# A graph network on one core: one-hot rows of the histogram stage laid out tile by tile, and half of one of them built on ScalarE

## The chip, the cores and the metric

The kernel runs on one core of a Trainium2 chip. The metric is device time in microseconds for one execution. The kernel before was timed three times: median 5992.08 us, 5985.56 to 5997.7 us. TensorE multiplies, VectorE and ScalarE work elementwise, GpSimd here mostly issues indirect DMAs, and a sync engine issues plain DMAs. Each engine runs its own instruction stream, and the streams meet at semaphores.

## The reference

Four graph layers run in sequence over the same graph: 6250 nodes with 128 features, and 106250 edges sorted by destination. A layer normalization and a relu stand ahead of each layer. What matters here is only how the graph is used. Layer 0, cut to its sum:

```
h = x @ w_in + b_in
Wij = (ssp(f_ij @ w_f1 + b_f1) @ w_f2 + b_f2) * rcut_ij[:, None]
x_ij = h[idx_j] * Wij
agg = segment_sum(x_ij, idx_i)
```

Layer 1 (a graph convolution) needs the sum of the edge weights at each destination node:

```
deg = segment_sum(ew, dst)
dinv = where(deg > 0, rsqrt(deg), 0.0)
norm = dinv[src] * ew * dinv[dst]
```

To sum by source, the kernel sorts the edges by source on the chip. For that it first counts how many edges each source node has.

## The kernel before

A node number is split into a block (number divided by 128, 49 blocks) and a lane (the remainder, 0 to 127). The edges lie in 832 tiles of 128, one edge per partition. Eight tiles are a group (`G = 8`), so there are 104 groups.

The stages follow one another, each with semaphores of its own, and a barrier of all engines stands between two of them. The first is `setup` (L125). The second is `histograms` (L201), which the change touches; after it come `rows_of_ends`, layer norm statistics, node tables, and the edge stage of layer 0, `filter_edges` (L621).

The histogram stage makes two results from one loop over the 104 groups, written as 52 turns of two halves `h`:

- The counts by source. For each tile there is a one-hot matrix of the source's block, `oh_hi` (128 edges by 49), and one of its lane, `oh_lo` (128 edges by 128). Their product over the edges, added up over all 832 tiles in the PSUM tile `p_count`, holds the count of edges of every source node. Before, `oh_lo` is the stationary operand and `oh_hi` the moving one, so `p_count` is lane by block (128x49). After the loop it is copied out and transposed to block by lane.
- The weight sums by destination. `d_lo` is the one-hot of the destination's lane. For each tile it is multiplied by six columns `w3` (the edge weight for the tile's first block or the next, each split in three bf16 parts). ScalarE copies the result of a group, 48 columns, from `p_deg` into `parts` (`keep`, L395).

VectorE makes all three one-hots of a group (L270, L272, L274): it compares a table of lane numbers with the node numbers. `oh_lo` and `d_lo` are stored lane-major, `[P, 2, P, G]`: the eight tiles of a group lie side by side for each lane. The table for that, `lanes16`, holds each lane number eight times (L177), and one tile's one-hot is read by TensorE at a stride of eight elements. `oh_hi` is stored tile-major.

Order and waits: VectorE may start group g once the weight sums of group g - 2 have left TensorE (`free`). TensorE waits for `oh_lo` (`src_hot`), multiplies eight tiles of counts (L347), waits for `d_lo` (`dst_hot`) and for ScalarE's copy of group g - 2 (`deg_kept`), and multiplies eight tiles of sums (L352). ScalarE waits for these and copies.

After the loop VectorE takes the counts (L277, L279), scans them (L280), and reduces `parts` (L287). The sync engine loads all weights during the loop (L386). GpSimd has nothing to do in this stage.

In `filter_edges` the same one-hots of the source are made again, tile-major, by `source_hots` (L832):

```
nc.vector.tensor_tensor(out=oh_lo[:, h], in0=K.lane16[:].unsqueeze(1).broadcast_to([P, G, P]),
                        in1=K.src_lo16[:, cols].unsqueeze(2).broadcast_to([P, G, P]), op=ALU.is_equal).then_inc(hot_ready, 1)
```

ScalarE's rows that the prediction uses are these forms: L510 is a Relu with bias and scale both read per partition; L782 and L784 are an Abs and a Relu of a PSUM tile with such a bias; L788 is an Ln of an SBUF tile with such a bias; L803 is a scaled copy from PSUM with such a scale.

Of the kernel before, what the change touches and what calls it, by code (L numbers as in the profile page):

```python
# [23 lines left out]
BF16 = mybir.dt.bfloat16  # L24
# [7 lines left out]
P = 128  # L32
# [6 lines left out]
G = 8  # L39
# [85 lines left out]
def setup(nc, A, K, s):  # L125

    loaded, made, tidy, blank, lanes = s.sem("loaded"), s.sem("made"), s.sem("tidy"), s.sem("blank"), s.sem("lanes")
    with nc.Block() as block:
# [29 lines left out]
        def _(dve):  # L158
# [18 lines left out]
            nc.vector.tensor_copy(K.lanes16[:], K.lane[:].unsqueeze(2).broadcast_to([P, P, G]))  # L177
# [5 lines left out]
            nc.vector.tensor_copy(K.dst_lo16[:], K.low_i[:])  # L183
            nc.vector.tensor_copy(K.dst_blk[0:1, :], K.key_i[0:1, :])
# [16 lines left out]
def histograms(nc, K, Dr, A, s):  # L201
# [4 lines left out]
    oh_lo = s.sb("oh_lo", [P, 2, P, G], BF16)  # L206
    d_lo = s.sb("d_lo", [P, 2, P, G], BF16)
    by_lane = s.sb("by_lane", [P, NB])
# [18 lines left out]
    src_hot, dst_hot, free, lane_counts, counts_turned = s.sem("src_hot"), s.sem("dst_hot"), s.sem("free"), s.sem("lane_counts"), s.sem("counts_turned")  # L227
# [15 lines left out]
    with nc.Block() as block:  # L243
        @block.vector
        def _(dve):
# [20 lines left out]
            with nc.vector.Fori(0, NG // 2) as i:  # L266
                for h in range(2):
                    cols = bass.ds(i * 2 * G + h * G, G)
                    dve.wait_ge(free, i * 2 + h + 1)
                    nc.vector.tensor_tensor(out=oh_hi[:, h], in0=K.lane16[:, 0:NB].unsqueeze(1).broadcast_to([P, G, NB]),  # L270
                                            in1=K.src_hi16[:, cols].unsqueeze(2).broadcast_to([P, G, NB]), op=ALU.is_equal)
                    nc.vector.tensor_tensor(out=oh_lo[:, h], in0=K.lanes16[:],  # L272
                                            in1=K.src_lo16[:, cols].unsqueeze(1).broadcast_to([P, P, G]), op=ALU.is_equal).then_inc(src_hot, 1)
                    nc.vector.tensor_tensor(out=d_lo[:, h], in0=K.lanes16[:],  # L274
                                            in1=K.dst_lo16[:, cols].unsqueeze(1).broadcast_to([P, P, G]), op=ALU.is_equal).then_inc(dst_hot, 1)
            dve.wait_ge(summed, 1)
            nc.vector.tensor_copy(by_lane[:], p_count[:, 0:NB]).then_inc(lane_counts, 1)  # L277
            dve.wait_ge(counts_turned, 1)
            step(dve, nc.vector.tensor_copy(count[:], p_count[0:NB, P:2 * P]), 1)  # L279
# [50 lines left out]
        def _(pe):  # L330
            pe.sem_inc(free, 2)
            pe.wait_ge(zeroed, 1)
            nc.tensor.matmul(p_count[:, 0:NB], zero[:], zero[:, 0:NB], start=True, stop=False, skip_group_check=True)
# [57 lines left out]
        def _(act):  # L391
# [2178 lines left out]
```

## Time and profile before

| | |
|---|---|
| median of three runs | 5992.08 us |
| the profiled execution, its own time | 5992.08 us |
| its span, first to last instruction | 5990.8 us |
| histogram loop in the trace | 32 to 211 us |
| VectorE busy in 32 to 210.7 us | 177.16 of 178.7 us |
| TensorE busy there | 163.49 us |
| ScalarE busy there | 20.55 us |

The profiled execution took 1.3 us more than its span. Busy time is time in which an instruction was under way on the engine; on VectorE and ScalarE consecutive instructions overlap by a little, so a sum of durations is more than the time that passes, and the distance between two starts is the better measure of what an instruction costs in a row of others. `hist_`, `c_`, `e_` and `k_` ahead of a tile's name say in which stage's memory it lies.

### The profile page before, as it was taken

What the parts mean: (1) busy time and instruction counts of PE and PEld (TensorE: products, weight loads), DVE (VectorE), ACT (ScalarE), POOL (GpSimd) and SP (SyncE); (2) the same over time, 40 slices, a digit from 0 to 9 for tenths busy, and PEclk for the clock granted to TensorE, in tenths of its full rate; (3) what the DMA queues carried; (4) which work ended last, traced back from release to release, by engine and by line L of the source; (5) the groups of instructions that cost most, each with busy time, mean ns of one, the idle gap of its engine ahead of it and who ended that gap; (6) DMA issues with size and microseconds to landing.
All of it is one profiled execution on the core that took longest, in us unless ns stands there. A gap on an engine that the chain in (4) does not pass through costs nothing. (4 is left out here: it accounts for less than half of the span.)

```text
span 5990.8 us, 102085 instructions
## 1 busy us (share of the span) xinstructions
PE 3458.2 (58%) x21282; PEld 2671.2 (45%) x21283; DVE 3512.1 (59%) x8519; ACT 1720.2 (29%) x3922; POOL 3789.8 (63%) x3879
## 2 busy tenths in 40 slices
PE   7768888888797333333354444444146645556556
PEld 7646666666575333333342222222136534344434
DVE  9858888888697433333355555555554454444444
ACT  0235555555344000000022333333157621111112
POOL 0077777777572677777707777777235437777774
PEclk9779999999897555555575555555579978766787
DMA  3099999999462121122228999999657622222221
GB/s 93 17 256 274 276 281 283 279 286 281 124 156 69 54 53 52 53 53 52 53 71 282 290 291 291 291 291 291 127 162 202 177 63 57 58 58 58 58 58 53
DMA packets 937028, 939.38 MB, mean 157 GB/s; under 512 B 330232, under 2 KB 777930, under 8 KB 936842
## 3 DMA queue, kind: packets, MB, share of 16 engines
q1 hardware_dynamic: 770906, 549.05, 34.0%
q0 software_dynamic: 137776, 369.86, 19.3%
q10 hardware_dynamic: 28288, 19.84, 1.1%
q8 instruction: 20, 0.33, 0.0%
q14 instruction: 38, 0.31, 0.0%
HBM read 686.22 MB, written 252.06 MB: 157 GB/s over the span
## 5 line engine op out<-in xcount | busy, mean ns | idle before, releaser
L1583 POOL DMA_INDIRECT edges_kv<-kv,edges_idx x880 | 836.5, 951 | 408.3 <-issue 267.8
L951 POOL DMA_INDIRECT by_src<-edges_rows,edges_pos x832 | 899.2, 1081 | 268.0 <-issue 257.2
L2213 POOL DMA_INDIRECT sum_rows<-table,sum_idx x832 | 806.2, 969 | 348.6 <-issue 253.2
L1310 POOL DMA_INDIRECT sum_rows<-table,sum_idx x832 | 788.1, 947 | 367.7 <-issue 251.4
L1387 PE MATMUL sum_p_sum<-sum_hot,sum_rows 128*128 128x128 f32 x1664 | 388.4, 427 | 662.4 <-DMA sum_rows<-table,sum_idx 662.4
L1387 PEld LDWEIGHTS sum_p_sum<-sum_hot,sum_rows 128*128 128x128 f32 x1664 | 360.4, 329 | 690.6 <-issue 690.6
L2311 PE MATMUL sum_p_sum<-sum_hot,sum_msg 128*128 128x128 f32 x1664 | 370.4, 414 | 466.7 <-DVE a_acc L2272 460.5
L1682 DVE TENSOR_TENSOR edges_kv<-edges_kv,edges_p_e 128x512 f32<-128x512 f32 x440 | 282.7, 684 | 530.4 <-DMA edges_kv<-kv,edges_idx 514.5
L2311 PEld LDWEIGHTS sum_p_sum<-sum_hot,sum_msg 128*128 128x128 f32 x1664 | 344.4, 315 | 552.9 <-issue 552.9
L1366 DVE TENSOR_TENSOR a_acc<-a_acc,sum_p_sum 128x128 f32 x832 | 234.3, 282 | 547.6 <-PE sum_p_sum L1387 546.4
L723 PE MATMUL edges_p_attr<-k_wekv,edges_attr 128*128 128x256 f32 x1664 | 467.0, 429 | 118.4 <-ACT edges_rows L798 114.6
L1713 PE MATMUL edges_p_q<-q_q,edges_src_hotT 128*128 x2640 | 373.0, 286 | 109.7 <-issue 86.7
L2257 DVE TENSOR_TENSOR sum_msg<-sum_p_msg,sum_rows 128x512 f32<-128x512 f32 x208 | 133.9, 685 | 493.5 <-DMA sum_rows<-table,sum_idx 493.5
L723 PEld LDWEIGHTS edges_p_attr<-k_wekv,edges_attr 128*128 128x128 f32 x1664 | 335.7, 212 | 174.6 <-ACT edges_rows L798 125.4
L1896 POOL TENSOR_TENSOR sum_wv<-sum_vv,sum_wv 128x1024 f32<-128x1024 f32 x110 | 212.5, 1932 | 313.6 <-ACT sum_wv L1911 312.1
L1623 ACT COPY edges_p_e<-edges_ekv 128x512 f32<-128x512 f32 x440 | 258.8, 589 | 463.6 <-DVE edges_kv L1682 446.6
L798 ACT COPY edges_rows<-edges_p_attr 128x512 f32<-128x512 f32 x416 | 223.4, 585 | 538.5 <-DMA by_src<-edges_rows,edges_pos 508.0
L1713 PEld LDWEIGHTS edges_p_q<-q_q,edges_src_hotT 128*128 128x128 bf16 x2640 | 274.8, 104 | 231.0 <-issue 172.9
L1349 DVE TENSOR_SCALAR sum_hot<-k_lane,k_dst_f,k_ew 128x128 f32<-128x128 f32 x832 | 304.2, 367 | 88.8 <-issue 88.3
L1723 PE MATMUL edges_p_l<-k_ident,edges_score 128*64 128x128 f32 x110 | 43.2, 392 | 498.7 <-DVE edges_score L1690 498.7
L1325 ACT COPY sum_idx<-k_src_i 128x8 int32 (+1 forms) x104 | 20.2, 197 | 989.9 <-DMA sum_rows<-table,sum_idx 984.0
L2272 DVE TENSOR_TENSOR a_acc<-a_acc,sum_p_sum 128x128 f32 x832 | 239.2, 288 | 99.6 <-DVE a_acc L2272 6.3
(381 smaller groups left out, 7781.6 us busy)
## 6 DMA issues: line engine op xcount, KB each, us to landing
edges_ekv<-by_src SPq DMA_DIRECT2D x110, 1024.0 KB
v<-edges_kv SPq DMA_DIRECT2D x110, 512.0 KB, 4.1
sum_vv<-v SPq DMA_DIRECT2D x110, 512.0 KB, 4.0
edges_attr<-in_attr128T SPq DMA_DIRECT2D x104, 512.0 KB
edges_near<-h_in SPq DMA_DIRECT2D x832, 48.0 KB
sum_rows<-by_src SPq DMA_DIRECT2D x110, 264.0 KB, 3.0
edges_src_b<-rel SPq DMA_DIRECT2D x110, 256.0 KB
edges_dst_b<-dst SPq DMA_DIRECT2D x104, 256.0 KB
```

The lines of the kernel that those rows point to most:

```text
L723: mm = nc.tensor.matmul(p_attr[:, c % 2, j, :], attr[:, q, (2 * c + j) * P:(2 * c + j + 1) * P], K.wekv[:], start=True, stop=True)
L951: nc.gpsimd.indirect_dma_start(Dr.by_src0, bass.IndirectOffsetOnAxis(pos[:, q, j:j + 1], 0), rows[:, q % 2, j, :], None).then_inc(scattere ...
L1310: nc.gpsimd.indirect_dma_start(rows[:, q, j, :], None, Dr.table, bass.IndirectOffsetOnAxis(idx[:, q, j:j + 1], 0)).then_inc(fetched[q], 16)
L1349: ins = nc.vector.tensor_scalar(hot[:, h, j, :], K.lane[:, 0:P], to, weight, ALU.is_equal, ALU.mult)
L1387: mm = nc.tensor.matmul(p_sum[:, c, j % 4, :], rows[:, q, j, :], hot[:, h, j, :], start=True, stop=True)
L1583: nc.gpsimd.indirect_dma_start(kv[:, q, j, :], None, Dr.kv, bass.IndirectOffsetOnAxis(idx[:, q, j:j + 1], 0)).then_inc(fetched[q], 16)
L1623: nc.scalar.copy(p_e[:, c % 2], ekv[:, q, 2 * c:2 * c + 2, :]).then_inc(e_ready, 1)
L1682: nc.vector.tensor_tensor(out=both, in0=both, in1=p_e[:, c % 2], op=ALU.add).then_inc(kv_ready, 1)
L1713: mm = nc.tensor.matmul(p_q[:, h, c, j % C, :], shot[:, h, j * P:(j + 1) * P], K.q[:, bass.ds(blk[j], 1), k, :].rearrange("p a d -> p (a d)"),
L2213: nc.gpsimd.indirect_dma_start(rows[:, q, j, :], None, Dr.table, bass.IndirectOffsetOnAxis(idx[:, q, j:j + 1], 0)).then_inc(fetched[q], 16)
L2272: nc.vector.tensor_tensor(out=place, in0=place, in1=p_sum[h][:, j // 4, j % 4, :], op=ALU.add).then_inc(added, 1)
L2311: mm = nc.tensor.matmul(p_sum[h][:, c, j % 4, :], msg[:, h, j, :], hot[:, h, j, :], start=True, stop=True)
```

## The change

The one-hots `oh_lo` and `d_lo` become tile-major, `[P, 2, G, P]`, so that a tile's one-hot is contiguous. The lane table that they are compared with is the plain 128-element one, repeated over the tiles, and the node numbers are repeated along the last dimension. `lanes16` and its making go.

In the count product the operands change places: `oh_hi` (49 columns) is stationary and `oh_lo` (128 columns) moves, so `p_count` is block by lane as it is needed, and the copy and the transpose behind the loop go.

VectorE makes `d_lo` for the first four tiles of a group only. For the other four ScalarE computes max(0, 1 - |lane - destination lane|), which is 1 where they are equal and 0 elsewhere: four Abs with the negated destination lane as bias into `far`, a wait for them, and one Relu of 512 columns (`near`). The negated lanes, `minus_lo`, are made once in the set-up. TensorE waits for both makers (`near_ready` is new). ScalarE makes its part of group g + 1 ahead of its copy for group g.

```diff
-            nc.vector.tensor_copy(K.lanes16[:], K.lane[:].unsqueeze(2).broadcast_to([P, P, G]))
...
             nc.vector.tensor_copy(K.dst_hi[:], K.key_i[:])
             nc.vector.tensor_copy(K.dst_lo16[:], K.low_i[:])
+            nc.vector.tensor_scalar(K.minus_lo[:], K.low_i[:], -1.0, None, ALU.mult)
             nc.vector.tensor_copy(K.dst_blk[0:1, :], K.key_i[0:1, :])
...
-    oh_lo = s.sb("oh_lo", [P, 2, P, G], BF16)
-    d_lo = s.sb("d_lo", [P, 2, P, G], BF16)
-    by_lane = s.sb("by_lane", [P, NB])
+    oh_lo = s.sb("oh_lo", [P, 2, G, P], BF16)
+    d_lo = s.sb("d_lo", [P, 2, G, P], BF16)
+    far = s.sb("far", [P, 2, G // 2, P])
...
                     cols = bass.ds(i * 2 * G + h * G, G)
+                    half = bass.ds(i * 2 * G + h * G, G // 2)
                     dve.wait_ge(free, i * 2 + h + 1)
                     nc.vector.tensor_tensor(out=oh_hi[:, h], in0=K.lane16[:, 0:NB].unsqueeze(1).broadcast_to([P, G, NB]),
                                             in1=K.src_hi16[:, cols].unsqueeze(2).broadcast_to([P, G, NB]), op=ALU.is_equal)
-                    nc.vector.tensor_tensor(out=oh_lo[:, h], in0=K.lanes16[:],
-                                            in1=K.src_lo16[:, cols].unsqueeze(1).broadcast_to([P, P, G]), op=ALU.is_equal).then_inc(src_hot, 1)
-                    nc.vector.tensor_tensor(out=d_lo[:, h], in0=K.lanes16[:],
-                                            in1=K.dst_lo16[:, cols].unsqueeze(1).broadcast_to([P, P, G]), op=ALU.is_equal).then_inc(dst_hot, 1)
+                    nc.vector.tensor_tensor(out=oh_lo[:, h], in0=K.lane16[:].unsqueeze(1).broadcast_to([P, G, P]),
+                                            in1=K.src_lo16[:, cols].unsqueeze(2).broadcast_to([P, G, P]), op=ALU.is_equal).then_inc(src_hot, 1)
+                    nc.vector.tensor_tensor(out=d_lo[:, h, 0:G // 2], in0=K.lane16[:].unsqueeze(1).broadcast_to([P, G // 2, P]),
+                                            in1=K.dst_lo16[:, half].unsqueeze(2).broadcast_to([P, G // 2, P]), op=ALU.is_equal).then_inc(dst_hot, 1)
             dve.wait_ge(summed, 1)
-            nc.vector.tensor_copy(by_lane[:], p_count[:, 0:NB]).then_inc(lane_counts, 1)
-            dve.wait_ge(counts_turned, 1)
-            step(dve, nc.vector.tensor_copy(count[:], p_count[0:NB, P:2 * P]), 1)
+            step(dve, nc.vector.tensor_copy(count[:], p_count[0:NB, 0:P]), 1)
...
-                        nc.tensor.matmul(p_count[:, 0:NB], oh_lo[:, h, :, j], oh_hi[:, h, j, :], start=False, stop=False, skip_group_check=True)
+                        nc.tensor.matmul(p_count[0:NB, 0:P], oh_hi[:, h, j, :], oh_lo[:, h, j, :], start=False, stop=False, skip_group_check=True)
                     pe.wait_ge(dst_hot, i * 2 + h + 1)
+                    pe.wait_ge(near_ready, i * 2 + h + 1)
                     pe.wait_ge(deg_kept, i * 2 + h + 1)
                     pe.sem_inc(tick, 1)
                     for j in range(G):
-                        mm = nc.tensor.matmul(p_deg[:, h, j * 6:(j + 1) * 6], d_lo[:, h, :, j],
+                        mm = nc.tensor.matmul(p_deg[:, h, j * 6:(j + 1) * 6], d_lo[:, h, j, :],
                                               w3[:, bass.ds(i * 2 * G + h * G + j, 1), :, :].rearrange("p a r m -> p (a r m)"), start=True, stop=True)
                     mm.then_inc(free, 1)
             pe.wait_ge(free, NG + 2)
             pe.sem_inc(summed, 1)
-            pe.wait_ge(lane_counts, 1)
-            nc.tensor.transpose(p_count[0:NB, P:2 * P], by_lane[:], K.ident[:]).then_inc(counts_turned, 1)
...
+            def near(g, h):
+
+                act.wait_ge(free, g + 1)
+                for j in range(G // 2):
+                    ins = nc.scalar.activation(far[:, h, j, :], K.lane[:], ACT.Abs, bias=K.minus_lo[:, bass.ds(g * G + G // 2 + j, 1)])
+                ins.then_inc(far_ready, 1)
+                act.wait_ge(far_ready, g + 1)
+                nc.scalar.activation(d_lo[:, h, G // 2:G, :], far[:, h], ACT.Relu, bias=K.ones[:, 0:1], scale=-1.0).then_inc(near_ready, 1)
+
             def keep(g, h):
...
-            with nc.scalar.Fori(0, NG // 2) as i:
+            near(0, 0)
+            with nc.scalar.Fori(0, NG // 2 - 1) as i:
                 for h in range(2):
+                    near(i * 2 + h + 1, 1 - h)
                     keep(i * 2 + h, h)
+            near(NG - 1, 1)
+            for h in range(2):
+                keep(NG - 2 + h, h)
```

VectorE's stream in one half of a turn of the histogram loop, with the shape that is written (`e_lane` is `lane16`, `c_lanes` is `lanes16`), before:

```order
L270 ISA
L270 TENSOR_TENSOR hist_oh_hi<-e_lane,e_src_hi 128x392
L272 REGISTER_ALU
L272 TENSOR_TENSOR hist_oh_lo<-c_lanes,e_src_lo 128x1024
L274 REGISTER_ALU
L274 TENSOR_TENSOR hist_d_lo<-c_lanes,c_dst_lo 128x1024
```

The same place now:

```order
L271 ISA
L271 TENSOR_TENSOR hist_oh_hi<-e_lane,e_src_hi 128x392
L273 REGISTER_ALU
L273 TENSOR_TENSOR hist_oh_lo<-e_lane,e_src_lo 128x1024
L275 REGISTER_ALU
L275 TENSOR_TENSOR hist_d_lo<-e_lane,c_dst_lo 128x512
```

There are still three compares per group; the second reads the other lane table, the third too and is half as long.

ScalarE's stream from its table load to the end of the first half of a loop turn, before:

```order
L393 ACT_TABLE_LOAD
L400 UNCONDITIONAL_BRANCH
L400 ISA
L398 ISA [waits hist_free]
L398 COPY hist_parts<-hist_p_deg 128x48
```

The first half of a loop turn now:

```order
L397 ISA [waits hist_free]
L397 ACTIVATE hist_far<-k_lane,c_minus_lo 128x128
L397 ISA
L397 ACTIVATE hist_far<-k_lane,c_minus_lo 128x128
L397 ISA
L397 ACTIVATE hist_far<-k_lane,c_minus_lo 128x128
L397 ISA
L397 ACTIVATE hist_far<-k_lane,c_minus_lo 128x128
L400 ACTIVATE hist_d_lo<-hist_far,k_ones 128x512 [waits hist_far]
L404 REGISTER_ALU
L405 ISA [waits hist_free]
L405 COPY hist_parts<-hist_p_deg 128x48
```

Five activations of the next group now stand ahead of each copy, and no table load stands among them.

## Rows read from the trace of the kernel before

**Rows 1.** The page: span; busy us (share) xinstructions of each engine.
```profile
span 5990.8 us, 102085 instructions
...
PE 3458.2 (58%) x21282; PEld 2671.2 (45%) x21283; DVE 3512.1 (59%) x8519; ACT 1720.2 (29%) x3922; POOL 3789.8 (63%) x3879
```

**Rows 2.** Busy time by stretch: start:end us, length, each engine, TensorE clock, DMA share, GB/s.
```profile
32.00:210.70 178.70, 163.49 (x1664) 157.80 (x1664) 177.16 (x313) 20.55 (x103) 0.00 (x0) 1.00 0.15 39
210.70:233.00 22.30, 10.80 (x51) 8.13 (x51) 15.09 (x32) 2.59 (x5) 0.00 (x0) 0.83 0.00 1
233.00:300.00 67.00, 41.90 (x178) 36.68 (x178) 53.24 (x176) 20.77 (x57) 0.00 (x0) 0.50 0.15 40
900.00:1530.00 630.00, 533.73 (x4180) 394.47 (x4178) 524.30 (x1673) 345.31 (x906) 486.49 (x453) 0.95 0.93 274
3139.00:4249.00 1110.00, 485.99 (x2964) 319.42 (x2964) 583.86 (x866) 326.87 (x760) 836.49 (x880) 0.50 0.92 285
```

**Rows 3.** The histogram loop's groups, 32 to 211 us; columns as the page's part 5.
```profile
L352 PE MATMUL hist_p_deg<-hist_w,hist_d_lo 128*128 x832 | 110.8, 220 | 0.1
...
L347 PE MATMUL hist_p_count<-hist_oh_hi,hist_oh_lo 128*128 128x49 bf16 x832 | 72.2, 241 | 25.4 <-issue 13.8 <-DVE hist_oh_lo L272 11.7
L272 DVE TENSOR_TENSOR hist_oh_lo<-c_lanes,e_src_lo 128x1024 bf16<-128x1024 bf16 x104 | 71.1, 684 | 0.0
L274 DVE TENSOR_TENSOR hist_d_lo<-c_lanes,c_dst_lo 128x1024 bf16<-128x1024 bf16 x104 | 71.1, 684 | 0.0
...
L270 DVE TENSOR_TENSOR hist_oh_hi<-e_lane,e_src_hi 128x392 bf16<-128x392 bf16 x104 | 58.6, 563 | 0.0
L398 ACT COPY hist_parts<-hist_p_deg 128x48 f32 x104 | 20.7, 200 | 174.2 <-PE hist_p_deg L352 174.2
```

**Rows 4.** Timeline of the loop, 207 to 212 us: start us, us, engine, line, what.
```profile
207.36 0.20 ACT L398 COPY hist_parts<-hist_p_deg 128x48 f32 x1 [1.47 <-PE hist_p_deg L352]
207.40 0.56 DVE L270 TENSOR_TENSOR hist_oh_hi<-e_lane,e_src_hi 128x392 bf16<-128x392 bf16 x1
...
207.49 0.69 PE L347 MATMUL hist_p_count<-hist_oh_hi,hist_oh_lo 128*128 128x49 bf16 x8 [0.27 <-issue]
207.88 0.68 DVE L272 TENSOR_TENSOR hist_oh_lo<-c_lanes,e_src_lo 128x1024 bf16<-128x1024 bf16 x1
...
208.01 0.96 PE L352 MATMUL hist_p_deg<-hist_w,hist_d_lo 128*128 x8
208.48 0.68 DVE L274 TENSOR_TENSOR hist_d_lo<-c_lanes,c_dst_lo 128x1024 bf16<-128x1024 bf16 x1
...
209.10 0.20 ACT L398 COPY hist_parts<-hist_p_deg 128x48 f32 x1 [1.54 <-PE hist_p_deg L352]
...
209.46 1.17 PE L352 MATMUL hist_p_deg<-hist_w,hist_d_lo 128*128 x8
210.76 0.21 DVE L277 COPY hist_by_lane<-hist_p_count 128x49 f32<-128x49 f32 x1 [1.60 <-PEq L356]
210.78 0.20 ACT L398 COPY hist_parts<-hist_p_deg 128x48 f32 x1 [1.48 <-PE hist_p_deg L352]
...
211.51 0.28 DVE L279 COPY hist_count<-hist_p_count 49x128 f32<-49x128 f32 x1 [0.54 <-PE hist_p_count L358]
```

**Rows 5.** Waits of ScalarE and of the DMA-issuing queue, start to 234 us.
```profile
ACT hist_parts L398 <- PE hist_p_deg L352: 172.7, 103, 19.4
...
SPq L243 <- PEq L243: 160.2, 1, 160.2
```

**Rows 6.** One line each, L272 and L837: durations ns min/median/max, first and last start.
```profile
L272 DVE TENSOR_TENSOR hist_oh_lo<-c_lanes,e_src_lo x104: 680/684/687, 32.5 to 207.9; 128x1024 bf16<-128x1024 bf16 x104
...
L837 DVE TENSOR_TENSOR edges_src_lo_hot<-e_lane,e_src_lo x104: 1209/1218/1222, 307.9 to 1503.6; 128x1024 bf16<-128x1024 bf16 x104
```

**Rows 7.** Timeline of VectorE in the edge loop, around 1503 us.
```profile
1503.09 0.56 DVE L835 TENSOR_TENSOR edges_src_hi_hot<-e_lane,e_src_hi 128x392 bf16<-128x392 bf16 x1
1503.57 1.22 DVE L837 TENSOR_TENSOR edges_src_lo_hot<-e_lane,e_src_lo 128x1024 bf16<-128x1024 bf16 x1
1504.70 0.48 DVE L844 TENSOR_SCALAR edges_dst_hotT<-edges_dst_b,k_node_col 128x1024 bf16<-128x1024 bf16 x1
```

**Rows 8.** ScalarE's groups over the whole span, shapes apart.
```profile
L1623 ACT COPY edges_p_e<-edges_ekv 128x512 f32<-128x512 f32 x440 | 258.8, 589 | 463.6 <-DVE edges_kv L1682 446.6 <-DMA edges_src_b<-rel 11.0 <-ACT edges_logit L1616 4.3
...
L1923 ACT COPY sum_p_sum<-sum_none 128x408 f32<-128x408 f32 x222 | 111.4, 502 | 85.5 <-DVE den_sums L1970 74.0 <-DVE sum_none L1952 7.9
...
L788 ACT ACTIVATE edges_ln<-edges_mag,k_ones 128x512 f32<-128x512 f32 x104 | 75.1, 722 | 3.4
...
L510 ACT ACTIVATE nodes_h<-k_x,k_shift,k_rstd 128x128 f32<-128x128 f32 x98 | 38.8, 481 | 6.3 <-PE nodes_p_t L551 4.1 <-PEq L487 2.2
```

**Rows 9.** Timelines of ScalarE: 257 us, and 423 to 428 us.
```profile
257.40 4.72 ACT L510 ACTIVATE nodes_h<-k_x,k_shift,k_rstd 128x128 f32<-128x128 f32 x12 [1.10 <-PEq L487]
...
423.67 1.77 ACT L803 ACTIVATE edges_w_cut<-edges_p_w,k_ew 128x64 f32<-128x64 f32 x8
425.25 0.76 ACT L782 ACTIVATE edges_mag<-edges_p_z,k_b_f 128x512 f32<-128x512 f32 x1
425.82 0.77 ACT L784 ACTIVATE edges_relu<-edges_p_z,k_b_f 128x512 f32<-128x512 f32 x1
426.39 0.71 ACT L786 ACTIVATE edges_mag<-edges_mag 128x512 f32<-128x512 f32 x1
427.14 0.72 ACT L788 ACTIVATE edges_ln<-edges_mag,k_ones 128x512 f32<-128x512 f32 x1
427.77 1.05 ACT L798 COPY edges_rows<-edges_p_attr 128x512 f32<-128x512 f32 x2
```

**Rows 10.** Timeline of TensorE at 3302 us, clock 0.50: 128-column moving rows.
```profile
3302.71 3.49 PE L1713 MATMUL edges_p_q<-q_q,edges_src_hotT 128*128 x24 [1.05 <-issue]
```

**Rows 11.** Timeline of VectorE in the set-up, 11 to 14 us.
```profile
11.10 0.68 DVE L177 CAST c_lanes<-k_lane 128x1024 bf16<-128x1024 f32 x1
11.70 0.58 DVE L179 TENSOR_SCALAR c_key_i<-k_dst_i 128x832 int32<-128x832 int32 x1
...
13.33 0.59 DVE L183 CAST c_dst_lo<-c_low_i 128x832 bf16<-128x832 int32 x1
13.83 0.57 DVE L184 COPY k_dst_blk<-c_key_i 1x832 int32<-1x832 int32 x1
```

More of the change, by code:

```diff
@@ L226, in histograms @@
     p_count, p_small, p_deg = s.ps("p_count", [P, 512]), s.ps("p_small", [P, 512]), s.ps("p_deg", [P, 2, 512])
-    src_hot, dst_hot, free, lane_counts, counts_turned = s.sem("src_hot"), s.sem("dst_hot"), s.sem("free"), s.sem("lane_counts"), s.sem("counts_turned")
+    src_hot, dst_hot, far_ready, near_ready, free = s.sem("src_hot"), s.sem("dst_hot"), s.sem("far"), s.sem("near"), s.sem("free")
     deg_kept, split, tick = s.sem("deg_kept"), s.sem("split"), s.sem("tick")
@@ L332, in _ @@
             pe.wait_ge(zeroed, 1)
-            nc.tensor.matmul(p_count[:, 0:NB], zero[:], zero[:, 0:NB], start=True, stop=False, skip_group_check=True)
+            nc.tensor.matmul(p_count[0:NB, 0:P], zero[:, 0:NB], zero[:], start=True, stop=False, skip_group_check=True)
             pe.wait_ge(blk_row, 1)
@@ L2476, in build @@
                 K.key_i, K.low_i = c.sb("key_i", [P, T], I32), c.sb("low_i", [P, T], I32)
-                K.dst_hi, K.dst_lo16 = c.sb("dst_hi", [P, T]), c.sb("dst_lo16", [P, T], BF16)
-                K.lanes16 = c.sb("lanes16", [P, P, G], BF16)
+                K.dst_hi, K.minus_lo, K.dst_lo16 = c.sb("dst_hi", [P, T]), c.sb("minus_lo", [P, T]), c.sb("dst_lo16", [P, T], BF16)
                 with Space(nc, "setup") as s:
```

## The prediction

> **What bounds the kernel now.** I read the page first: 5990.8 us of span, with no engine over 63% busy [rows 1]. That average covers stages with different limits, and the change touches one only, so the second view is the table of busy time by stretch. In the histogram loop, 32 to 210.7 us, VectorE is busy 177.16 of 178.70 us, TensorE 163.49, ScalarE 20.55 and GpSimd not at all [rows 2]. VectorE has no gap there, so it is the bound, with TensorE not far behind.
>
> The third view is the groups of the loop. VectorE has three compares per group, 104 of each, of 563, 684 and 684 ns, each with 0.0 us of idle time ahead of it [rows 3]. Their sum, 1.93 us, is more than what passes, because instructions in a row overlap. The timeline shows what each costs from start to start: 207.40 to 207.88 is 0.48 us for `oh_hi`, then 0.60 us to 208.48 for `oh_lo` [rows 4]. `d_lo` takes the same 684 ns, so about 0.61. That is 1.69 us. Over the loop, the first `oh_lo` starts at 32.5 and the last at 207.9 [rows 6], so 175.4 us over 103 groups is 1.703 us per group. I use 1.703: the three compares and about 0.01 us of loop turn.
>
> ScalarE waits for TensorE's sums 172.7 of these 179 us [rows 5]; it has much time to give. The sync engine's loads are not late: its queue then waits 160.2 us at the stage's barrier for others [rows 5]. Stages are parted by barriers, so whatever this loop loses or wins goes into the total one to one, unless a later stage changes its own pace.
>
> **The compares in the new layout.** This is the term that decides. VectorE's `oh_hi` isn't changed: 0.48 us. The new `oh_lo` doesn't stand in this loop's trace, but it stands in the edge loop's: L837 has the same operands, the same tile-major output, and the node number repeated along the last dimension. It takes 1218 ns (1209 to 1222, 104 times), against 684 ns (680 to 687) for the lane-major form of the same 1024 elements [rows 6]. From its start to the next instruction is 1503.57 to 1504.70, 1.13 us, against 0.60 [rows 7, 4]. Could L837 be slow because of what runs beside it, such as GpSimd's indirect DMAs? Its neighbour L835 has the form of `oh_hi` and takes 0.56 us there and 0.56 us here, where GpSimd is idle [rows 7, 4, 2]; and L837's spread of 13 ns over a long stage with all kinds of neighbours shows no such share. So the layout costs +0.53 us per group.
>
> The new `d_lo` on VectorE has the same form with 512 elements. The line through 560 ns at 392 and 1218 ns at 1024 elements [rows 7, 6] has 1.04 ns per element; 512 elements come to 0.685 us, less the 0.08 us by which L835's duration is more than its distance of 0.48: 0.60 us. Its ends: half of 1.13 is 0.57 (no fixed part), and 0.48 x 512 / 392 is 0.63 (nothing but a fixed rate). I take 0.60, the line between two rows of its own form. So halving `d_lo` wins nothing: half the elements at about twice the price each.
>
> Together: 0.48 + 1.13 + 0.60 + 0.01 = 2.22 us per group, against 1.703. From unrounded numbers I take 2.22; ends 2.19 and 2.25. Times 104 groups: +53.8 us, ends +50.6 and +56.9.
>
> **ScalarE's new part.** Per group four Abs of 128 columns with one per-partition bias, a wait for them, a Relu of 512 columns, and the old copy. The nearest row for a 512-column activation from SBUF with one such operand is L788, 722 ns; copies of 512 and 408 columns take 589 and 502 ns, 0.837 ns per column [rows 8]. An Abs of 128 columns is then 722 - 384 x 0.837 = 401 ns. Two activations from SBUF in a row overlap by 0.096 us: 12 of L510 take 4.72 us, so (4.72 - 0.48) / 11 = 0.385 apart, at 481 ns each [rows 9, 8]. So an Abs every 0.305 us: 3 x 0.305 + 0.401 = 1.32. The wait for its own result costs 0.04 (426.39 + 0.71 = 427.10, next start 427.14), the Relu 0.63 until the next start (427.14 to 427.77) [rows 9], and the copy 0.200 - 0.096 = 0.10 [rows 3]. Sum: 2.09 us per group. That is under VectorE's 2.22, so it is hidden, but by 0.13 us only.
>
> Its ends. Below: eight of L803, 64 columns, take 1.77 us, 0.204 apart, and 64 more columns make 0.257; with the 0.57 us between L782 and L784 for the Relu [rows 9] it is 0.77 + 0.40 + 0.04 + 0.57 + 0.10 = 1.89. Above: L510 itself, the only 128-column activation from SBUF, at 0.385 and 0.481, though it reads two per-partition operands, and no overlap elsewhere: 1.16 + 0.48 + 0.04 + 0.72 + 0.20 = 2.60. I take 2.09, whose terms have the right number of operands. The register step ahead of each Abs costs nothing extra: L803 has one too, at 0.204 us.
>
> Here the Trainium skill bears on the choice. L510 shows 481 ns and L788 722 ns [rows 8]. "ScalarE: Activation LUTs", in its section on what ACT_TABLE_LOAD costs, says that an activation with one per-partition pointer takes about 280 ns + 0.833 ns per column, that each further pointer adds about 93 ns, and that those in a row overlap by about 93 ns. By that, as an estimate, L510 is 480 and L788 706, so the trace agrees within 16 ns; an Abs is 387, one every 294, and the group 3 x 0.294 + 0.387 + 0.04 + 0.61 + 0.10 = 2.02. Neither it nor my rows make ScalarE the bound; only L510's spacing, taken over with its second operand, would.
>
> Does ScalarE's turn fit in time? Its part for group g + 2 may start when the sums of group g are done and copied, about 1.2 us after VectorE's `d_lo` of g (208.48 + 0.68 = 209.16, sums end at 210.63 [rows 4]; with the count product in front, up to 1.5). It is done 2.0 us later, at +3.5 at most, and TensorE needs it when VectorE's `d_lo` of g + 2 is ready, at +4.4. So TensorE's new wait is nearly always met. What queues behind it, the sums, `free` and so VectorE's group g + 3, has 0.9 us of room.
>
> **TensorE.** Before: 0.69 us for eight count products, 0.96 to 1.17 for eight sums [rows 4]. Now the count product moves 128 columns, not 49, over 49 columns of weights. The nearest row of 128 moving bf16 columns is L1713, at clock 0.50 (1.2 GHz): 24 in 3.49 us, (3.49 - 0.29) / 23 = 0.139 us each [rows 10, 2]. Eight: 1.11 us at most; at the clock of 1.00 (2.4 GHz) that the loop has [rows 2] nearer the 0.69 of now. The sums read contiguous weights and get no slower: at most 1.17. Together 1.65 to 2.28; I take 1.8, hidden under 2.22. Relief for TensorE wins nothing, as it isn't the bound.
>
> **Small terms.** Behind the loop the copy and the transpose go: `count` is taken at the time of `by_lane`, so 211.51 - 210.76 = -0.75 us, all on the path [rows 4]. In the set-up the lane table goes (11.10 to 11.70, -0.60) and `minus_lo` comes, 832 elements as L183 (13.33 to 13.83, +0.50) [rows 11]: -0.10.
>
> **Sum.** +53.8 - 0.75 - 0.10 = +53.0 us on the profiled execution's 5992.08 us, which is also the median of the runs: 6045 us, +0.9%.
>
> **Rivals.**
> 1. *ScalarE becomes the bound.* For: its sum lies only 0.13 us under VectorE's, and it has semaphore and register steps in the chain. Against: it needs the second operand's price, or 0.04 us per instruction more than I count. With L510's spacing alone: 1.16 + 0.40 + 0.04 + 0.63 + 0.10 = 2.33 us, times 104 against 1.703 is +65.2, so 6056. At its upper end of 2.60, +93.3, so 6084. TensorE's upper end of 2.28 would lead to 6051 in the same way.
> 2. *Not slower: the new layout keeps the old rate.* Place: the compare of 1024 elements. If it took 0.60 us here and its half about 0.35, VectorE would need 1.44 us, and the loop's pace would pass to ScalarE and TensorE. It would end level with before where these reach 1.70: TensorE can (1.65); ScalarE only if an Abs comes every 0.204 us as L803 does, 0.61 + 0.34 + 0.04 + 0.57 + 0.10 = 1.66. Then 5991. Against: L837's 1209 to 1222 ns, 104 times, and ScalarE's lower end of 1.89, with which this still costs +19 and ends at 6011.
> 3. *A later stage gives it back or adds to it.* TensorE does less in this loop, and its clock afterwards could be another. Against: the clock falls to 0.50 behind the loop now, in 233 to 300 us, and is 0.95 in the long edge loop [rows 2]; there is nothing left to gain there. A few us either way.
>
> **How the numbers follow.** Forecast 0.74; rival 1, 0.20; rival 2, 0.03; rival 3 with more than 40 us, 0.03, half of it to either side. The forecast's own range is +50 to +57 from the loop, with 6 us for the spread of runs: 6037 to 6054. The range given, 6036 to 6068, takes in most of rival 1 and leaves out its upper end. A measurement of this kernel can tell about 0.2% (12 us) from no change. Faster 0.015, same 0.03, slower 0.955.
>
> **What would show it.** In the new trace: `oh_lo` at 1.21 to 1.22 us and the half `d_lo` at 0.67 to 0.70; VectorE still without gaps, about 2.22 us per group; durations on ScalarE that add up to about 2.5 us per group (overlaps counted twice), waiting a little for TensorE's sums each time; the loop from 32 to about 264 us; `near_ready` hardly waited for. If VectorE waits for `free` in each group and ScalarE has no wait, rival 1 is right. If `oh_lo` takes 0.69, the main term is wrong.

## The result, and the profile after

The changed kernel takes 6040.28 us (median of 6 runs, 6035.44 to 6043.26) against 5991.54 us before (6 runs, 5984.08 to 5997.7). The ratio is 1.008 with a 95% interval of 1.0068 to 1.0091: slower by 49 us, 41 to 55. The forecast was 6045 us, or +53.

The profiled execution took 6046.61 us, +54.5 to the one before. Its page, span and busy time by engine [rows 1]:

```profile
span 6045.4 us, 103159 instructions
...
PE 3497.4 (58%) x21281; PEld 2674.7 (44%) x21282; DVE 3568.2 (59%) x8518; ACT 1911.0 (32%) x4442; POOL 3799.9 (63%) x3879
```

By stretch, as in [rows 2]: the loop, the two stretches behind it, and the long edge loop, 55 us later than before:

```profile
32.00:264.00 232.00, 203.42 (x1664) 158.49 (x1664) 230.71 (x313) 209.88 (x613) 0.00 (x0) 1.00 0.12 31
264.00:287.00 23.00, 13.55 (x52) 11.04 (x51) 13.15 (x25) 2.59 (x5) 0.00 (x0) 1.00 0.00 1
287.00:354.00 67.00, 41.89 (x178) 36.67 (x178) 53.34 (x180) 20.76 (x57) 0.00 (x0) 0.60 0.14 37
955.00:1585.00 630.00, 544.20 (x4143) 401.83 (x4139) 522.23 (x1662) 340.89 (x893) 486.62 (x449) 0.93 0.93 272
```

Two things are to be seen. VectorE is busy 230.71 of 232 us in a loop that was 178.7 us long, and ScalarE went from 20.55 to 209.88 us. Little moved elsewhere: TensorE's clock is still 1.00 in the loop, and 0.93 in the long edge loop, where it was 0.95. Behind the loop it stays up for longer, 1.00 and then 0.60 where 0.83 and 0.50 were granted before [rows 2], but no time came of it (see below).

The loop's groups [rows 3], from 15 to 290 us, columns as in the page's part 5:

```profile
L397 ACT ACTIVATE hist_far<-k_lane,c_minus_lo 128x128 f32<-128x128 f32 x416 | 132.8, 391 | 12.8 <-issue 12.8
L273 DVE TENSOR_TENSOR hist_oh_lo<-e_lane,e_src_lo 128x1024 bf16<-128x1024 bf16 x104 | 127.1, 1222 | 0.0
L346 PE MATMUL hist_p_count<-hist_oh_lo,hist_oh_hi 128*49 128x128 bf16 x832 | 109.0, 311 | 38.7 <-DVE hist_oh_lo L273 38.7
...
L400 ACT ACTIVATE hist_d_lo<-hist_far,k_ones 128x512 bf16<-128x512 f32 x104 | 75.1, 722 | 3.4
L275 DVE TENSOR_TENSOR hist_d_lo<-e_lane,c_dst_lo 128x512 bf16<-128x512 bf16 x104 | 71.6, 689 | 0.0
```

`oh_lo` went from 684 to 1222 ns, and half a `d_lo` costs 689 ns where the whole cost 684. VectorE has still 0.0 us of idle time ahead of each compare. A stretch of the loop [rows 4], start and duration in us:

```profile
121.37 1.22 DVE L273 TENSOR_TENSOR hist_oh_lo<-e_lane,e_src_lo 128x1024 bf16<-128x1024 bf16 x1
...
121.91 0.72 ACT L400 ACTIVATE hist_d_lo<-hist_far,k_ones 128x512 bf16<-128x512 f32 x1
122.50 0.69 DVE L275 TENSOR_TENSOR hist_d_lo<-e_lane,c_dst_lo 128x512 bf16<-128x512 bf16 x1
122.55 0.20 ACT L405 COPY hist_parts<-hist_p_deg 128x48 f32 x1
...
122.73 1.05 PE L346 MATMUL hist_p_count<-hist_oh_lo,hist_oh_hi 128*49 128x128 bf16 x8 [0.30 <-DVE hist_oh_lo L273]
123.01 1.28 ACT L397 ACTIVATE hist_far<-k_lane,c_minus_lo 128x128 f32<-128x128 f32 x4 [0.26 <-issue]
123.11 0.56 DVE L271 TENSOR_TENSOR hist_oh_hi<-e_lane,e_src_hi 128x392 bf16<-128x392 bf16 x1
123.58 1.22 DVE L273 TENSOR_TENSOR hist_oh_lo<-e_lane,e_src_lo 128x1024 bf16<-128x1024 bf16 x1
...
123.71 0.95 PE L352 MATMUL hist_p_deg<-hist_w,hist_d_lo 128*128 x8
```

VectorE's starts are 1.13 us (`oh_lo` to `d_lo`), 0.61 (`d_lo` to `oh_hi`) and 0.47 apart: 2.21 us per group. All 104 `oh_lo`, with durations in ns (min/median/max) and the first and last start [rows 6]:

```profile
L273 DVE TENSOR_TENSOR hist_oh_lo<-e_lane,e_src_lo x104: 1218/1222/1224, 32.8 to 260.9; 128x1024 bf16<-128x1024 bf16 x104
```

So (260.9 - 32.8) / 103 = 2.215 us per group, against 1.703. Behind the loop [rows 4]:

```profile
264.31 0.28 DVE L278 COPY hist_count<-hist_p_count 49x128 f32<-49x128 f32 x1 [1.60 <-PEq L356]
...
265.51 5.34 DVE L286 TENSOR_REDUCE hist_by_tile<-hist_parts 128x1664 f32<-128x4992 f32 x1
```

The same reduction in the kernel before:

```profile
212.71 5.33 DVE L287 TENSOR_REDUCE hist_by_tile<-hist_parts 128x1664 f32<-128x4992 f32 x1
```

It starts at 265.51 us against 212.71: +52.8 us up to there. From its start to the end of the span it is 5779.9 us against 5778.1: the later stages add no more than 1.8 us.

The waits from 40 to 250 us, with the total, the number and the longest:

```profile
PE hist_p_count L346 <- DVE hist_oh_lo L273: 24.5, 95, 0.3
...
ACT hist_far L397 <- issue: 12.0, 47, 0.3
```

TensorE waits for `oh_lo` in every group. ScalarE has no wait for TensorE in the list, only 0.26 us of "issue" (waiting for nothing that the profile shows) in every second group. `near_ready` holds nobody: the Relu of the group whose sums start at 121.42 us had ended at 120.61.

### The profile page after: what moved, and what is told of

Read it like the earlier page. It is cut to its first block and busy times, and to the rows that moved or that the text cites. A ratio compares the mean times of both kernels' runs of the same rounds, so it can differ in the third digit from the quotient of the medians.

```text
span 6045.4 us, 103159 instructions
## 1 busy us (share of the span) xinstructions
PE 3497.4 (58%) x21281; PEld 2674.7 (44%) x21282; DVE 3568.2 (59%) x8518; ACT 1911.0 (32%) x4442; POOL 3799.9 (63%) x3879
## 5 line engine op out<-in xcount | busy, mean ns | idle before, releaser
L1378 DVE TENSOR_TENSOR a_acc<-a_acc,sum_p_sum 128x128 f32 x832 | 235.6, 283 | 549.3 <-PE sum_p_sum L1399 548.2
L2013 PE MATMUL sum_p_sum<-sum_wv,sum_hot 128*128 128x136 f32 x1760 | 235.8, 288 | 107.5 <-ACT sum_p_sum L1935 59.0
```

The costliest lines, as they stand in the source:

```text
L2013: mm = nc.tensor.matmul(p_sum[:, h, c, bass.ds(slot[j], 1), :].rearrange("p a f -> p (a f)"), hot[:, h, j, :], wv[:, q, j, :], start=False ...
```

## Experiments

For each, the pace of the loop is worked out as above: the first and the last start of `oh_lo`, over 103 groups. The table has it beside the times, all medians in us.

| run | us per group | time before the same runs | time | ratio, 95% |
|---|---|---|---|---|
| before | 1.703 | | 5991.54 | |
| changed | 2.215 | 5991.54 | 6040.28 | 1.0080 (1.0068 to 1.0091) |
| layout only | 2.748 | 5994.40 | 6101.36 | 1.0180 (1.0164 to 1.0195) |
| half only | 3.593 | 5994.40 | 6184.94 | 1.0320 (1.0304 to 1.0336) |
| five on ScalarE | 2.396 | 5994.40 | 6067.70 | 1.0127 (1.0111 to 1.0142) |
| two on ScalarE, lane-major | 2.099 | 5994.40 | 6028.94 | 1.0060 (1.0046 to 1.0073) |
| swap only | 2.503 | 5980.69 | 6066.26 | 1.0143 (1.0126 to 1.0160) |
| pairs in the changed kernel | 2.004 | 5993.11 | 6026.30 | 1.0053 (1.0037 to 1.0068) |
| pairs, old operands, two on ScalarE | 1.674 | 5993.11 | 5984.06 | 0.9986 (0.9977 to 0.9995) |
| pairs for `oh_hi` only | 1.606 | 5993.11 | 5983.92 | 0.9987 (0.9978 to 0.9996) |

The kernel before was timed again with each series of runs, and the series ran on different chips, so times are compared within a row only. The pace before comes from one trace. The pace accounts for the time to within 6.3 us: for "layout only" (2.748 - 1.703) x 103 = 107.6 us, measured 107.0; for "swap only" 82.4, measured 85.6; for "pairs in the changed kernel" 31.0, measured 33.2; for "five on ScalarE" 71.4, measured 73.3; for "pairs for `oh_hi` only" -10.0, measured -9.2. It is 4 to 6 us off for the changed kernel (52.7, measured 48.7), "half only" (194.7, measured 190.5), "two on ScalarE, lane-major" (40.8, measured 34.5) and "pairs, old operands" (-3.0, measured -9.1). What differs there behind the loop was not looked for.

**Layout only.**

```diff
-  d_lo[:, h, 0:G // 2] compared on VectorE; d_lo[:, h, G // 2:G] made by near()
+  d_lo[:, h] compared on VectorE, tile-major, 1024 elements
-                    pe.wait_ge(near_ready, i * 2 + h + 1)
```

> The changed kernel with ScalarE's part taken out: VectorE makes all eight tiles of d_lo in the tile-major layout, TensorE waits for it alone, ScalarE only copies. Theory (VectorE sets the pace, and the layout doubles the price of a compare): 0.48 + 1.13 + 1.13 + 0.01 = 2.75 us per group against 1.703, so +109 us less 0.75 behind the loop: 6100 us, 60 us over the changed kernel. Rival (the layout is not what costs, ScalarE's part set the changed kernel's pace): the loop gets no slower than the changed kernel's 2.21 us per group, or falls back to about 1.7: 5990 to 6040 us.

VectorE's timeline:

```profile
120.54 1.22 DVE L273 TENSOR_TENSOR hist_oh_lo<-e_lane,e_src_lo 128x1024 bf16<-128x1024 bf16 x1
121.67 1.22 DVE L275 TENSOR_TENSOR hist_d_lo<-e_lane,c_dst_lo 128x1024 bf16<-128x1024 bf16 x1
122.81 0.56 DVE L271 TENSOR_TENSOR hist_oh_hi<-e_lane,e_src_hi 128x392 bf16<-128x392 bf16 x1
```

Both compares take 1.13 us from start to start, and 2.748 us per group and +107 us were measured where 2.75 and 6100 were expected. The layout is the cost, and moving half of `d_lo` away bought back (2.748 - 2.215) x 103 = 55 us of it. This run keeps the exchanged operands of the count product too, but VectorE has no wait in it, so they have no part in its pace. Nor does ScalarE's work slow VectorE much: the median `oh_lo` takes 1215 ns here and 1222 ns beside it.

**Half only.**

```diff
+  d_lo[:, h, :, 0:G - S] compared on VectorE, lane-major, S = 4
+  nc.scalar.activation(d_lo[:, h, :, G - S:G].rearrange("p l j -> p j l"), far[:, h], ACT.Relu, ...)
+                    pe.wait_ge(near_ready, i * 2 + h + 1)
```

> The kernel before with ScalarE's part alone: lane-major layout and its tables stay, VectorE compares the first four tiles of d_lo (512 elements), ScalarE makes the other four as in the changed kernel but writes them at a stride of eight elements. VectorE then needs about 0.48 + 0.61 + 0.35 = 1.44 us per group and ScalarE sets the pace, so this measures ScalarE's own pace. Theory (ScalarE has slack in the changed kernel, 2.02 to 2.09 us per group): +33 to +40 us, 6025 to 6032 us. Rival (the changed kernel's ScalarE has no slack, its idle 0.26 us at every second group is the loop's turn and not a wait): 2.21 us per group, +52 us, 6044 us, the same as the changed kernel. If half a d_lo on ScalarE were free: 5991 or less.

Neither theory held. ScalarE's timeline:

```profile
119.79 0.53 ACT L413 COPY hist_parts<-hist_p_deg 128x48 f32 x1
120.00 1.30 ACT L405 ACTIVATE hist_far<-k_lane,c_minus_lo 128x128 f32<-128x128 f32 x4
121.33 2.60 ACT L408 ACTIVATE hist_d_lo<-hist_far,k_ones 128x512 bf16<-128x512 f32 x1
123.44 0.53 ACT L413 COPY hist_parts<-hist_p_deg 128x48 f32 x1
```

ScalarE does set the pace, but at 3.59 us: the Relu takes 2.60 us where the changed kernel's takes 0.722. The copy's 0.53 us, for 0.20, is mostly overlap, since it starts 0.49 us before the Relu's recorded end (121.33 + 2.60 = 123.93). From start to start, Relu to copy is 2.11 us, for 0.63, and copy to Abs 0.21, for 0.08. The only difference of the two Relus is that this one writes bf16 at a stride of eight elements. So this run did not measure what it was made for; it measured the price of a strided write.

**Two on ScalarE, lane-major.** The same kernel with `S = 2`.

> The kernel before with two of the eight tiles of d_lo on ScalarE, in the lane-major layout. ScalarE: 0.305 + 0.40 + 0.04 + 0.63 - 0.21 + 0.10 = 1.27 us per group, hidden. VectorE: 0.48 + 0.61 + 768 elements in the fast form, about 0.48 = 1.57 us against 1.703, so -14 us: 5978 us. Rival (TensorE, with its strided weight loads, takes the pace at once): 1.65 us or more, -5 us or no change. If the compare of six neighbouring tiles loses the fast form (768 elements at the other rate, 0.87 us): 1.96 us, +27 us.

It went the wrong way, by +35 us where -14 were expected, for the same reason. Its Relu of 256 columns, strided, and that of the later run "pairs, old operands, two on ScalarE", the same instruction with a contiguous output (busy us, mean ns of one, idle before):

```profile
L408 ACT ACTIVATE hist_d_lo<-hist_far,k_ones 128x256 bf16<-128x256 f32 x77 | 113.1, 1469 | 2.5
```

```profile
L416 ACT ACTIVATE hist_d_lo<-hist_far,k_ones 128x256 bf16<-128x256 f32 x84 | 42.7, 508 | 2.7
```

1469 against 508 ns. With 512 columns 2602 against 722: the strided write costs (2602 - 1469) / 256 = 4.4 ns per column, the contiguous one (722 - 508) / 256 = 0.84. ScalarE is not without gaps here: in every second group TensorE's sums start 0.28 us behind the Relu's end (120.48, then 120.76), and the copy 0.13 us behind the sums' end (121.92, then 122.05). So the 2.10 us are those of a chain through both engines, of which the strided Relu is the longest link.

**Five on ScalarE.**

```diff
-  far[P, 2, G // 2, P], four Abs, Relu of 512; VectorE compares four tiles
+  far[P, 2, 5, P], five Abs, Relu of 640; VectorE compares three tiles
```

> The changed kernel with five tiles of d_lo on ScalarE and three (384 elements) on VectorE. VectorE: 0.48 + 1.13 + 0.47 + 0.01 = 2.09 us per group. ScalarE: one Abs (0.305) and 128 columns of Relu (0.107) more than its pace. Theory (ScalarE at 2.05 to 2.09 in the changed kernel, hidden under VectorE's 2.21): 2.46 to 2.50 us per group, +26 to +30 us over the changed kernel, about 6068. Rival (ScalarE at 2.21 already): 2.62 us, +43 us, about 6083. If VectorE alone counted, it would be 12 us faster than the changed kernel: 6028.

```profile
120.48 1.57 ACT L398 ACTIVATE hist_far<-k_lane,c_minus_lo 128x128 f32<-128x128 f32 x5
122.08 0.83 ACT L401 ACTIVATE hist_d_lo<-hist_far,k_ones 128x640 bf16<-128x640 f32 x1
122.82 0.18 ACT L406 COPY hist_parts<-hist_p_deg 128x48 f32 x1
122.90 1.57 ACT L398 ACTIVATE hist_far<-k_lane,c_minus_lo 128x128 f32<-128x128 f32 x5
```

ScalarE now has no idle time: a copy, 0.08 us, five Abs and their wait to the Relu, 0.74 to the next copy. The pace is 2.396 us, +71 us by the loop and +73 measured. The theory's 2.46 to 2.50 was a little high, though its 6068 us was met (6067.70); the rival's 2.62 was wrong, and "VectorE alone counts" has the wrong sign. ScalarE becomes the bound between four tiles and five.

**Swap only.**

```diff
-                        nc.tensor.matmul(p_count[:, 0:NB], oh_lo[:, h, :, j], oh_hi[:, h, j, :], ...)
+                        nc.tensor.matmul(p_count[0:NB, 0:P], oh_hi[:, h, j, :], oh_lo[:, h, :, j], ...)
```

> The kernel before with only the count product's operands changed over: oh_hi stationary, oh_lo moving and still lane-major, so read at a stride of eight elements; the copy and the transpose behind the loop go. Theory: VectorE keeps the pace of 1.703 us per group, and the 0.75 us behind the loop go, which a measurement of the whole can't see: 5991 us. Rival: the strided moving read is slow, TensorE goes over 1.70 us per group and the loop follows it; at 2.0 us per group +31 us.

```profile
121.35 2.00 PE L345 MATMUL hist_p_count<-hist_oh_lo,hist_oh_hi 128*49 128x128 bf16 x8
...
121.57 0.57 DVE L270 TENSOR_TENSOR hist_oh_hi<-e_lane,e_src_hi 128x392 bf16<-128x392 bf16 x1 [0.75 <-PE hist_p_deg L350]
...
123.28 0.65 PE L350 MATMUL hist_p_deg<-hist_w,hist_d_lo 128*128 x8
```

The rival is right: eight count products with a moving operand read at a stride of eight take 2.00 us, where they take 1.05 from the contiguous one of the changed kernel. TensorE is busy without a gap, and VectorE waits for it. So the operand swap needs the new layout; alone it costs 86 us. The eight sums, with strided weights as in the kernel before, take 0.65 us here, where they took 0.96 to 1.17 [rows 4].

**The compare by itself.** Results that nobody reads, ahead of the loop. It was run once, for its durations; its time says nothing.

```diff
+  a: in0=K.lane16[:].unsqueeze(1).broadcast_to([P, G, P]), in1=K.src_lo16[:, 0:P].unsqueeze(1).broadcast_to([P, G, P])
+  b: the same, in1=K.src_lo16[:, k * G:(k + 1) * G].unsqueeze(2).broadcast_to([P, G, P])
+  c: nc.vector.tensor_scalar(scrap[:, 8, k, :], K.lane16[:], ref[:, k:k + 1], None, ALU.is_equal)
```

> The kernel before with twenty extra VectorE instructions ahead of the histogram loop, whose results nobody reads: four compares of 1024 elements tile-major with the second operand contiguous in the last dimension and repeated over the tiles (a), four with the second operand repeated along the last dimension (b, the changed kernel's form), eight compares of one tile of 128 lanes with a per-partition scalar (c). Theory (the repeat along the last dimension costs the rate, not the tile-major output): a 0.68 us, b 1.22 us, c about 0.15 to 0.25 us each. Rival (the shape of output or lane table costs it): a and b both 1.22 us.

```profile
31.99 2.48 DVE L268 TENSOR_TENSOR hist_scrap<-e_lane,e_src_lo 128x1024 bf16<-128x1024 bf16 x4
34.40 4.62 DVE L271 TENSOR_TENSOR hist_scrap<-e_lane,e_src_lo 128x1024 bf16<-128x1024 bf16 x4
38.94 1.39 DVE L274 TENSOR_SCALAR hist_scrap<-e_lane,k_dst_f 128x128 bf16<-128x128 bf16 x8
40.24 0.56 DVE L279 TENSOR_TENSOR hist_oh_hi<-e_lane,e_src_hi 128x392 bf16<-128x392 bf16 x1
```

Four of a take 34.40 - 31.99 = 2.41 us, 0.60 each; four of b 4.54, 1.13 each; eight of c 1.30, 0.16 each. a and b write the same tile-major output from the same lane table. What costs the rate is the node number repeated at stride zero in the last dimension, not the output's layout. c would need 1.30 us for eight tiles, more than 0.60 or 1.13.

**Pairs in the changed kernel.** Each lane number is stored twice, so that the last dimension is a run of two:

```diff
+  nc.vector.tensor_copy(to[:], of[:].unsqueeze(2).broadcast_to([P, T, 2]))
+  out.rearrange("p g (l k) -> p g l k", k=2), in1=numbers[:, cols, :].unsqueeze(2).broadcast_to([P, n, width // 2, 2])
```

> The changed kernel with the source and destination lanes stored twice each, so that the tile-major compares read the node number as a run of two neighbouring elements instead of one repeated at stride zero; the rest, ScalarE's half and TensorE's order, as changed. Three more lines ahead of the loop, partly in a wait, cost up to 1 us. Theory (the stride of zero in the last dimension costs the rate, and any run of two gives it back): oh_lo 0.68 us, the half d_lo 0.42, VectorE 0.48 + 0.61 + 0.34 = 1.43 us per group. The pace then goes to ScalarE (2.00 us by the run with five tiles, which has 2.41 less one tile's 0.41) and to TensorE (0.98 us for the counts and 1.07 for the sums of a group without a wait in that run, 2.05): 2.05 us per group, -17 us to the changed kernel, 6024 us. Rival (a run of two doesn't give the rate back): 2.21 us per group, 6040 us.

```profile
120.06 0.69 DVE L229 TENSOR_TENSOR hist_oh_lo<-e_lane,hist_src_lo 128x1024 bf16<-128x1024 bf16 x1
...
120.66 0.42 DVE L229 TENSOR_TENSOR hist_d_lo<-e_lane,hist_dst_lo 128x512 bf16<-128x512 bf16 x1
121.33 0.72 ACT L410 ACTIVATE hist_d_lo<-hist_far,k_ones 128x512 bf16<-128x512 f32 x1
121.59 0.57 DVE L283 TENSOR_TENSOR hist_oh_hi<-e_lane,e_src_hi 128x392 bf16<-128x392 bf16 x1 [0.51 <-PE hist_p_deg L362]
...
122.04 1.28 ACT L407 ACTIVATE hist_far<-k_lane,c_minus_lo 128x128 f32<-128x128 f32 x4
...
123.35 0.72 ACT L410 ACTIVATE hist_d_lo<-hist_far,k_ones 128x512 bf16<-128x512 f32 x1
```

The theory holds: `oh_lo` is back at 0.60 us from start to start and the half `d_lo` takes 0.42 us, tile-major both. VectorE now waits 0.5 us per group for TensorE's sums, and ScalarE, without a gap from one Abs group to the next (2.02 and 2.004 us on the mean), sets the pace. This is the measurement of ScalarE's own pace that "half only" failed to give: 2.00 us with four tiles, and 2.40 with five. It also shows that the layout was not the only thing wrong with the change: with the fast compare given back the kernel is still 33 us slower than before. Four tiles and the copy take ScalarE 2.00 us per group, where all eight tiles cost VectorE 0.61. TensorE, with the operands changed over, is close behind: from 40 to 190 us it is busy 138.45 of 150, so 1.85 us per group. Without ScalarE's part the pace might not fall below that; this was not run.

**Pairs, old operands, two on ScalarE.**

```diff
+  all three compares in pairs, oh_hi widened to 50 columns; oh_lo stationary as before; near() with S = 2
```

> A version meant to beat both: tile-major one-hots compared in pairs, all three of them (oh_hi widened to 50 columns), TensorE's count product with oh_lo stationary as before, two of eight tiles of d_lo on ScalarE. Theory: VectorE 0.28 + 0.61 + 0.47 = 1.36 us per group, ScalarE 2.00 - 2 x 0.41 = 1.18, TensorE 0.52 + 0.84 = 1.36 as in the kernel before when it doesn't wait: about 1.40 us, -31 us, and 2 to 3 us back for making the pairs: 5963 us against 5992. Rival (TensorE can't hold that pace): 1.65 us per group, -3 us or no change. If a run of two doesn't give the fast rate: over 2.2 us per group, +50 us.

```profile
120.72 0.37 DVE L231 TENSOR_TENSOR hist_oh_hi<-e_lane,hist_src_hi 128x400 bf16<-128x400 bf16 x1
...
120.87 0.51 PE L360 MATMUL hist_p_count<-hist_oh_hi,hist_oh_lo 128*128 128x49 bf16 x8 [0.30 <-issue]
121.01 0.69 DVE L231 TENSOR_TENSOR hist_oh_lo<-e_lane,hist_src_lo 128x1024 bf16<-128x1024 bf16 x1
...
121.27 1.16 PE L366 MATMUL hist_p_deg<-hist_w,hist_d_lo 128*128 x8
...
122.36 0.51 PE L360 MATMUL hist_p_count<-hist_oh_hi,hist_oh_lo 128*128 128x49 bf16 x8
```

VectorE's compares start 0.29 and 0.60 us apart, and it waits in every second group. On TensorE it is 0.40 us from the count products to the sums and 1.09 from the sums to the next counts, 1.49 in all, and 0.3 us of "issue" ahead of every second group. The rival holds for the pace: 1.674 us. The time is 0.14% under before (0.05 to 0.23), 9 us, of which the pace gives 3; where the rest comes from is not shown.

**Pairs for `oh_hi` only.** The kernel before, with `oh_hi` widened to 50 columns and compared in pairs.

> The kernel before with one compare changed: oh_hi widened to 50 columns and compared in pairs; oh_lo and d_lo stay lane-major, ScalarE only copies. Theory: oh_hi from 0.48 to 0.28 us, VectorE 1.49 us per group, TensorE follows at 1.36 to 1.50: -20 us, and 1 us for the pairs: 5972 us against 5992. Rival (TensorE, at a stride of eight for its weights, is the bound just under VectorE): 1.65 us per group, -5 us.

```profile
120.38 0.36 DVE L273 TENSOR_TENSOR hist_oh_hi<-e_lane,hist_src_hi 128x400 bf16<-128x400 bf16 x1
120.66 0.69 DVE L275 TENSOR_TENSOR hist_oh_lo<-c_lanes,e_src_lo 128x1024 bf16<-128x1024 bf16 x1
...
122.12 0.37 DVE L273 TENSOR_TENSOR hist_oh_hi<-e_lane,hist_src_hi 128x400 bf16<-128x400 bf16 x1 [0.18 <-PE hist_p_deg L355]
```

`oh_hi` takes 0.28 us from start to start, not 0.48. The loop's pace is 1.606 us, 10 us less over the loop, and 0.13% less were measured (0.04 to 0.22). That lies between theory and rival: of the 0.20 us per group that VectorE gives, 0.10 are won, and VectorE then waits 0.18 us for TensorE's sums in every second group. Of the versions run, these last two are the only ones with a time under both kernels; they can't be told from each other.

## Why the prediction was right

**The main term** held. Forecast 0.48 + 1.13 + 0.60 + 0.01 = 2.22 us per group, measured 2.215; forecast for `oh_lo` 1218 ns by the edge loop's row [rows 6], measured 1222; for the half `d_lo` 685, measured 689. "Layout only" gives the same price for a whole `d_lo`. That what runs beside the compare has no part in its price was argued from L835; the compare by itself, with GpSimd idle, takes 1.13 us too and shows it.

**Rival 2**, that the layout keeps the old rate, is refuted by the changed kernel, and the probe says on what it hangs: with a contiguous last dimension the same output takes the old 0.60 us. With that rate given back in pairs the pace was 2.004 us, not the 1.70 that the rival needed; ScalarE set it.

**ScalarE's part** was hidden, as forecast, and my sum of 2.09 us was 0.09 too high: "pairs in the changed kernel" has 2.00. So the room under VectorE was 0.21 us per group, not 0.13. The terms: four Abs take 1.28 us where I had 1.32, the Relu 0.62 to 0.64 (0.63), and from copy to Abs are 0.08 (0.10). The estimate by "ScalarE: Activation LUTs" of the Trainium skill, 2.02, was nearer: an Abs by it is 387 ns and the trace has 391 on the mean. Rival 1 at its upper ends (L510's 0.385 us spacing) is refuted: an Abs comes every 0.30 us. But its mechanism is real, and shows when a fifth tile is moved.

**Rival 3**: the later stages added 1.8 us; nothing of 40 us came from there. Its mechanism did show, though I had said that the clock had nothing left to gain: it is 1.00 and 0.60 in the two stretches behind the loop, for 0.83 and 0.50, and 0.93 for 0.95 in the edge loop.

**TensorE** I put at 1.8 us, within 1.65 to 2.28. In the changed kernel it has 0.98 from counts to sums and about 1.0 for the sums, so it was hidden, with 0.2 us less room than I thought. The term that was mis-sized is the count product: I expected the full clock to bring it near the 0.69 us of before, and it takes 1.05, close to the 1.11 worked out from the slower clock. So changing the operands over gave TensorE more work, not less; it did no harm only because VectorE's pace hides it. I had not considered that the moving operand's stride matters; in the changed kernel it is contiguous.

**The wait that was added** holds nobody, as forecast. Its sign in the trace was another than I said: ScalarE's slack, 2.215 - 2.004 = 0.21 us per group, appears in every second group between copy and Abs: 0.46 us from start to start (122.55 to 123.01, with 0.26 us of "issue"), for 0.08. The copy ahead of it starts 0.12 us behind the end of TensorE's sums (121.42 + 1.01 = 122.43), so this may be my wait in another guise; no run settles it.

**Small terms.** Behind the loop: from the end of the last sums to `count` it was 211.51 - 210.63 = 0.88 us [rows 4] and is 264.31 - 264.16 = 0.15 now, so 0.73 went, forecast 0.75. In the set-up VectorE started 0.41 us later, waiting for a load, which more than takes up the 0.10 gained there: the loop starts 0.31 us later. The sum of the profiled pair is +52.8 us up to the reduction, forecast +53.0; that the two agree to 0.2 us is in part luck, since the loop gave 52.7 where I had 53.8, and the set-up +0.3 where I had -0.1. The median's +49 is 4 us less. The profiled execution, 6046.61 us, is the slowest of all on record for the changed kernel, and no other has a trace, so where these 4 us lie is not shown.

## What to carry to other kernels

Look for the new form of an instruction elsewhere in the same trace before believing in a layout: one row with the same operands told the price to 0.3%. When a bf16 one-hot is made by a VectorE comparison, the repeated operand should be repeated in an outer dimension, or stored as pairs, not at stride zero in the last (0.60 us for 1024 elements, not 1.13); half the elements at twice the price is no saving. Work can be moved to an idle engine with a gain (55 us of 108 here), if its writes stay contiguous, but first ask what makes it dear where it is: at VectorE's fast rate the same move makes ScalarE the bound, at 2.00 us per group where the kernel before has 1.70.

## What the runs showed that was not expected

- A ScalarE activation that writes bf16 at a stride of eight elements takes 2602 ns for 512 columns and 1469 for 256, against 722 and 508 contiguous: 4.4 ns per column, not 0.84.
- TensorE's moving operand read at a stride of eight elements costs eight 128-column products 2.00 us, not 1.05. As the stationary operand the same stride costs little: eight products of 49 columns take 0.70 us strided in the kernel before, and 0.51 contiguous. With the same contiguous tiles and the operands changed over it is 1.05.
- A run of two elements in the last dimension is enough for VectorE's fast compare: 0.60 us for 1024 elements from start to start.
- Eight sums of six columns take about 1 us in most runs, whether their weights are strided (0.96 to 1.17 [rows 4]) or contiguous (0.89 to 1.17). But neither is a floor: behind the 2.00 us of count products in "swap only" they take 0.65, with strided weights, and in "pairs in the changed kernel", with contiguous ones, about 1.1 and 0.75 in turn. What holds them at 1 us is left open: each has a register step ahead of it, which might get done early behind a long count product; that is a guess, and no run took the step away.
